# Query, key and value turns of a transformer block written out and skewed over the engines, with the norms ahead of them on VectorE

## The reference, cut to what matters

```python
ada = t_emb @ w_ada + b_ada
sh_msa, sc_msa, g_msa, sh_mlp, sc_mlp, g_mlp = jnp.split(ada, 6, axis=-1)
xn = layer_norm(logmap0(x))
xm = expmap0(xn * (1 + sc_msa) + sh_msa)
q = _to_heads(plin(xm, w_q, b_q))        # plin: expmap0(logmap0(x) @ w + b)
k = _to_heads(plin(xm, w_k, b_k))        # 16 heads of 16 columns, each rescaled
v = _to_heads(plin(xm, w_v, b_v))
scores = jnp.einsum('bhqd,bhkd->bhqk', logmap0(q), logmap0(k)) / math.sqrt(HD)
...
x = x + _L0_cond_ref(x, cond_1024[:, None, :], ...)
x = x + _L1_cond_ref(x, cond_1024, Wx, Wh, b)     # LSTM, 512 steps
```

## Time and profile before

| | us |
|---|---|
| median of three runs | 1699.41 |
| lowest, highest | 1697.03, 1707.28 |
| profiled execution | 1704.82 |
| its span, first to last instruction | 1703.1 |
| TensorE, VectorE, ScalarE, GpSimd busy | 1504.9, 1182.9, 915.1, 466.2 |
| mean granted TensorE clock, share of full | 0.901 |

### The profile page before, as it was taken

How to read it: one execution, slowest core, us unless ns; L and a number is a source line. 1 busy time by engine, 2 the same in 40 slices (tenths; PEclk the granted TensorE clock), 3 DMA queues, 4 the chain that set the end, 5 groups by cost and what they waited for, 6 DMA issues and landing times.

```text
span 1703.1 us, 65744 instructions
## 1 busy us (share of the span) xinstructions
PE 1504.9 (88%) x25387; PEld 1261.3 (74%) x25387; DVE 1182.9 (69%) x6690; ACT 915.1 (54%) x3335; POOL 466.2 (27%) x1246
## 2 busy tenths in 40 slices
PE   3565658548999999999999999999999999999998
PEld 3444546437887888888888888888788888888887
DVE  6465657636888787868786868677766767676665
ACT  0334349627676666565656565657454454544433
POOL 4222220200515142515151515151513314140100
PEclk9767675567999999989998989899999999999999
DMA  8000000000000000000000000000000000000000
GB/s 247 0 0 0 0 0 2 1 1 5 3 3 10 3 10 3 9 3 9 8 5 7 5 9 3 9 3 9 3 9 3 9 3 9 6 3 6 3 6 6
DMA packets 16711, 18.39 MB, mean 11 GB/s; under 512 B 6037, under 2 KB 15385, under 8 KB 16409
## 3 DMA queue, kind: packets, MB, share of 16 engines
q1 hardware_dynamic: 13016, 10.51, 2.1%
q10 hardware_dynamic: 3392, 3.81, 0.8%
HBM read 12.21 MB, written 2.10 MB: 8 GB/s over the span
## 4 chain that ended last, share of the span: by engine, by line
PE 64%; DVE 10%; POOL 4%; ACT 4%; issue 4%; POOLq 0%; ACTq 0%; DVEq 0%
PE psum L784 22%; PE psum L822 19%; PE psum L760 4%; PE psum L725 4%; PE psum L732 3%; PE psum L660 3%; DVE weights L1146 2%; POOL sc L262 2%; PE psum L672 2%; PE psum L740 2%; PE psum L774 2%; ACT weights L895 1%; DVE gA L1386 1%; DVE gF L1388 1%; POOL sc L464 1%
## 5 line engine op out<-in xcount | busy, mean ns | idle before, releaser
L784 PEld LDWEIGHTS psum<-hl,wh 128*128 128x128 f16 x16384 | 480.3, 96 | 86.0 <-DVE hl L1404 74.6
L784 PE MATMUL psum<-hl,wh 128*128 128x8 f16 x16384 | 515.9, 172 | 5.8 <-DVE hl L1404 3.7
L822 PE MATMUL psum<-zeros,ident 128*128 128x256 f16 x3316 | 451.5, 276 | 7.4 <-DVE gF L1388 2.1
L822 PEld LDWEIGHTS psum<-zeros,ident 128*128 128x128 f16 x3316 | 304.8, 98 | 79.4 <-DVE gF L1388 17.9
L992 ACT ACTIVATE tA<-gA 128x16 f32<-128x16 f32 x512 | 110.4, 216 | 434.1 <-DVE gA L1386 433.6
L1146 DVE TENSOR_TENSOR weights<-w,weights 128x256 f16<-128x256 f32 x512 | 202.9, 418 | 18.7 <-ACT weights L895 18.4
L1386 DVE TENSOR_REDUCE gA<-psum 128x16 f32<-128x32 f32 x512 | 96.5, 189 | 148.3 <-PE psum L784 141.6
L901 ACT ACTIVATE w<-psum 128x512 f32<-128x512 f32 x256 | 154.4, 603 | 4.9 <-DVE weights L1146 4.5
L1402 DVE TENSOR_TENSOR hl<-ot 128x8 f16<-128x8 f32 x512 | 90.1, 176 | 95.1 <-ACT ot L998 94.9
L895 ACT ACTIVATE weights<-psum 128x512 f16<-128x512 f32 x256 | 153.6, 600 | 3.9 <-PE psum L672 3.9
L998 ACT ACTIVATE ot<-cnew 128x8 f32<-128x8 f32 x512 | 109.6, 214 | 81.6 <-DVE cnew L1395 31.9
(11 more groups left out here) (301 smaller groups left out, 2318.2 us busy)
## 6 DMA issues: line engine op xcount, KB each, us to landing
arena<-in_x_dram SPq DMA_DIRECT2D x4, 512.0 KB, 9.6
wf<-in_L_cond_w_f_dram SPq DMA_DIRECT2D x2, 1024.0 KB, 17.2
xr<-in_x_dram SPq DMA_DIRECT2D x64, 32.0 KB, 1.8
out_dram<-place SPq DMA_DIRECT2D x64, 32.0 KB, 1.6
qTs<-in_L_cond_w_ada_dram ACTq DMA_DIRECT2D x1, 1536.0 KB
oT<-in_L_cond_Wh_dram ACTq DMA_DIRECT2D x1, 1024.0 KB, 14.1
wx<-in_L_cond_Wx_dram SPq DMA_DIRECT2D x1, 1024.0 KB, 18.8
rows<-in_L_cond_b_ada_dram ACTq DMA_DIRECT2D x4, 128.0 KB, 14.4
```

Of the source, the lines that this page charges most:

```text
L784: last = mm(cols, wh16[:, half, kc, (g0 + c) * P:(g0 + c + 1) * P], hl[:, :, kc, :, 2].rearrange("p e b -> p b e"), start=False, stop=c == ...
L822: mm(pF[:, D:2 * D], ident16[:], zeros[:], start=False, stop=False, skip_group_check=True)
```

## The change

The start and the loop are rewritten; attention, recurrence and output stay, but for buffer names. Four groups of edits:

1. **Norms.** `to_ratio` and `to_norm` are gone from GpSimd. VectorE computes them in `norms(tiles, part)`, four parts for tiles 0 to 3 and four for tiles 4 to 15, laid between the statistics, which now have three `mv6` buffers and no wait after each. GpSimd computes four powers.
2. **Smaller start.** `adac` has only the two parts that the loop needs (8 products, not 24). The other uses of w_ada, the products for h0, the maximum of W_h over partitions and the units move into `between_turns` of the engines. W_h's high halves are ScalarE's (`high_half`, turns 4 to 11), the low halves VectorE's, one instruction each after the loop.
3. **Written out and skewed.** The loops become Python loops over turns -3 to 17. In turn t TensorE does heads t-2, linears t+1, transpose t+3, norm column t+2; ScalarE squares t, modulation t+2, norm t+3, roots t, copies t-2; VectorE linears t, row norm t+1, factors t-1, head sums t, halves t-1; GpSimd row factor t+1, values t-1. `lin` and `uT` have two buffers.
4. **Wider instructions.** `lin` is one instruction of 768 columns from three banks; the factors f are one; q and k are one of 512. TensorE waits only for ld_q (w_q, w_k, w_v) ahead of the linears, and the biases are loaded ahead of W_h. The table load for the attention is at turn 15.

```diff
+for i, ((lo, hi), which) in enumerate((tiles, which) for tiles in (FIRST_TILES, LAST_TILES) for which in (HALF_UP, HALF_DOWN)):
+    hold(pool, "q_in", i + 1)
+    w = hi - lo
+    g.tensor_tensor(num(f"ka{lo}", w), num(f"kb{lo}", w), cst[:, which, 0:w], ALU.pow).then_inc(s["q_out"], 1)
+ch = Chain(pool, s["hsc"], s["held"], 0)
+def tile_scale(k):
+    hold(pool, "p_ns", k + 1)
     clip(ch, num("su"), num("nu"), 1, num("ca"), num("cb"), s["p_su"])
+def values(k):
     hold(pool, "p_f", k + 1)
+    ch.link(g.tensor_scalar(num("fv", H), num("f", 48)[:, 2 * H:3 * H], V_UP, None, ALU.mult))
...
+    hold(pool, "p_v", k + 1)
     g.tensor_copy(vh, v32).then_inc(s["p_vh"], 1)
     hold(pool, "p_vh", k + 1)
     g.tensor_tensor(vl, v32, vh, ALU.subtract).then_inc(s["p_vl"], 1)
+for turn in range(-1, NT + 1):
+    if turn + 1 < NT:
+        tile_scale(turn + 1)
+    if 0 <= turn - 1:
+        values(turn - 1)
...
+for turn in range(-3, NT + 2):
+    if 0 <= turn - 2:
+        heads_turned(turn - 2)
+    if 0 <= turn + 1 < NT:
+        linears(turn + 1)
+    if turn + 3 < NT:
+        x_turned(turn + 3)
+    if 0 <= turn + 2 < NT:
+        row_norm(turn + 2)
+    between_turns(turn)
+pe.wait_ge(s["ld_w"], 16 * WLOADS)
+pe.wait_ge(s["h0_s"], 1)
+pe.wait_ge(s["p_kc"], NT)
+pe.wait_ge(s["p_qc"], NT)
...
+def between_turns(turn):
+    if turn == 0:
+        pe.wait_ge(s["pk"], 1)
+        tr(bank[6][0:1, 0:P], big1[:, 2:3], ident[:]).then_inc(s["wmax"], 1)
+    if turn == 1:
+        pe.wait_ge(s["pk"], 2)
+        mm(bank[6][:, 256:257], ones[0:1, :], big1[0:1, 4:5], start=True, stop=True, skip_group_check=True).then_inc(s["wmax"], 1)
+    if turn in (3, 4, 6, 7):
...
+        for kc in range(KD):
+            last = mm(GROUP_ROWS[i % 2], c0R[:, kc, :, :].rearrange("p b t -> p (b t)"), wada[:, kc, part * D:(part + 1) * D],
+                      start=kc == 0, stop=kc == KD - 1, skip_group_check=True)
+        last.then_inc(s["gp"], 1)
+    if 9 <= turn < 13:
+        if turn == 9:
+            pe.wait_ge(s["ld_h"], 16)
+            pe.wait_ge(s["gp_s"], 2)
+        for gi in (2 * (turn - 9), 2 * (turn - 9) + 1):
+            c = CHUNK[gi]
+            for kc in range(KD):
+                last = mm(bank[6][:, gi * B:(gi + 1) * B], wh[:, kc, c * P:(c + 1) * P], c0T[:, kc, :],
+                          start=kc == 0, stop=kc == KD - 1, skip_group_check=True)
+        last.then_inc(s["h0p"], 1)
...
+def high_half(gi):
+    c = CHUNK[gi]
+    if gi == 0:
+        act.wait_ge(s["unit_s"], 1)
+    A(wh16[:, 0, :, gi * P:(gi + 1) * P], wh[:, :, c * P:(c + 1) * P], ACT.Copy,
+      scale=big1[:, 6:7] if UNIT[gi] == 1.0 else big1[:, 5:6]).then_inc(s["w_hi"], 1)
+logs(FIRST_TILES, 1)
+normed(0)
+for turn in range(-2, NT + 2):
+    if 0 <= turn < NT:
+        squares(turn)
+    if turn + 2 < NT:
+        modulated(turn + 2)
+    if turn + 3 < NT:
+        normed(turn + 3)
+    if turn == -2:
+        logs(LAST_TILES, 2)
+    if 0 <= turn < NT:
+        roots(turn)
+    if turn == NT - 1:
+        nc.scalar.preload_act_table_set("exp_and_others")
+    if 0 <= turn - 2:
+        heads_kept(turn - 2)
+    if 4 <= turn < 4 + GC:
+        high_half(turn - 4)
...
+def norms(tiles, part):
+    lo, hi = tiles
...
+    if part == 1:
+        link(d.tensor_tensor(N("a"), m, m, ALU.mult))
+        link(d.tensor_tensor(N("c"), N("a"), var, ALU.add))
+        d.tensor_scalar(N("b"), N("c"), float(D), None, ALU.mult).then_inc(s["q_in"], 1)
+    if part == 2:
+        v.wait_ge(s["q_out"], 2 * number + 1)
...
+    if part == 3:
+        v.wait_ge(s["lnr"], number + 1)
+        link(d.scalar_tensor_tensor(N("lam"), N("L"), 0.5, N("ndi"), ALU.mult, ALU.mult))
...
+        d.tensor_scalar(N("b"), N("d"), LN_EPS, None, ALU.add).then_inc(s["q_in"], 1)
+    if part == 4:
+        v.wait_ge(s["q_out"], 2 * number + 2)
+        link(d.tensor_tensor(kap[:, lo:hi], N("lamf"), N("a"), ALU.mult))
+        d.scalar_tensor_tensor(kmn[:, lo:hi], kap[:, lo:hi], -1.0, m, ALU.mult, ALU.mult).then_inc(s["ln1"], 1)
...
+statistics(0, 4)
+norms(FIRST_TILES, 1)
+statistics(4, 6)
 v.wait_ge(s["c0t"], 1)
 d.tensor_copy(c0T[:], bank[0][:, 0:KD * B].rearrange("p (k b) -> p k b", b=B)).then_inc(s["c0t_s"], 1)
+norms(FIRST_TILES, 2)
+statistics(6, 8)
 v.wait_ge(s["c0t_s"], 1)
 d.tensor_copy(c0R, c0T[:].unsqueeze(3).to_broadcast([P, KD, B, RING])).then_inc(s["c0t_s"], 1)
+norms(FIRST_TILES, 3)
+statistics(8, 11)
+norms(FIRST_TILES, 4)
+statistics(11, NT)
+norms(LAST_TILES, 1)
+v.wait_ge(s["adap"], 1)
+link(d.tensor_tensor(adac[:], bank[1][:, 0:2 * KD * B].rearrange("p (c b) -> p c b", b=B),
+                     badac[:, 0:2 * KD].unsqueeze(2).to_broadcast([P, 2 * KD, B]), ALU.add))
+d.tensor_scalar(adac[:, KD:2 * KD, :], adac[:, KD:2 * KD, :], 1.0, None, ALU.add).then_inc(s["ada_s"], 1)
+norms(LAST_TILES, 2)
 v.wait_ge(s["ld_h"], 16)
+d.tensor_reduce(big1[:, 0:1], wh, axis=AX.XY, op=ALU.max)
+norms(LAST_TILES, 3)
 link(d.tensor_reduce(big1[:, 1:2], wh, axis=AX.XY, op=ALU.min))
 link(d.tensor_scalar(big1[:, 3:4], big1[:, 1:2], -1.0, 2.0 ** -60, ALU.mult, ALU.max))
 d.tensor_tensor(big1[:, 2:3], big1[:, 0:1], big1[:, 3:4], ALU.max).then_inc(s["pk"], 1)
...
+def linears(k):
+    v.wait_ge(s["p_mm"], k + 1)
+    v.wait_ge(s["p_su"], k + 1)
+    if k == 0:
+        v.wait_ge(s["ld_bq"], 16 * 3)
+    if k >= 2:
+        v.wait_ge(s["p_v"], k - 1)
+    d.scalar_tensor_tensor(lin_of(k), psum[:, 2:5, 0:D], num("su"), bqkv, ALU.mult, ALU.add).then_inc(s["p_lin"], 1)
...
+def factors(k):
+    v.wait_ge(s["p_r"], k + 1)
+    link(d.tensor_scalar(num("ct", 3), num("rss", 51)[:, 48:51], REACH * HEAD, HEAD, ALU.mult, ALU.min))
+    if k >= 1:
+        v.wait_ge(s["p_v"], k)
+    by_three = lambda t: t.rearrange("p (a h) -> p a h", a=3)
...
+    v.wait_ge(s["p_f"], k + 1)
+    by_head = lambda t: t.rearrange("p a (h e) -> p (a h) e", e=HD)
+    d.scalar_tensor_tensor(by_head(qk), by_head(lin_of(k)[:, 0:2, :]), QK_UP,
+                           num("f", 48)[:, 0:2 * H].unsqueeze(2).to_broadcast([P, 2 * H, HD]), ALU.mult, ALU.mult).then_inc(s["p_qk"], 1)
+def head_sums(k):
+    v.wait_ge(s["p_sq"], k + 1)
+    if k >= 1:
+        v.wait_ge(s["p_r"], k)
+    d.tensor_reduce(num("ss", 51)[:, 0:48], tmp[:, 0:3 * D].rearrange("p (h e) -> p h e", e=HD), axis=AX.X, op=ALU.add).then_inc(s["p_s1"], 1)
+    v.wait_ge(s["p_s1"], k + 1)
+    link(d.tensor_reduce(num("ss", 51)[:, 48:51], num("ss", 51)[:, 0:48].rearrange("p (a h) -> p a h", a=3), axis=AX.X, op=ALU.add))
+    d.tensor_scalar(num("ss", 51), num("ss", 51), 1.0, None, ALU.max).then_inc(s["p_ss"], 1)
...
+for turn in range(-1, NT + 1):
+    if 0 <= turn < NT:
+        linears(turn)
+    if turn + 1 < NT:
+        row_norm(turn + 1)
+    if 0 <= turn - 1:
+        factors(turn - 1)
+    if 0 <= turn < NT:
+        head_sums(turn)
+    if 0 <= turn - 1:
+        halves(turn - 1)
+    between_turns(turn)
+v.wait_ge(s["h0p"], 4)
+v.wait_ge(s["unit_s"], 1)
...
+v.wait_ge(s["w_hi"], GC)
+for gi, c in enumerate(CHUNK):
+    d.scalar_tensor_tensor(wh16[:, 1, :, gi * P:(gi + 1) * P], wh[:, :, c * P:(c + 1) * P],
+                           big1[:, 6:7] if UNIT[gi] == 1.0 else big1[:, 5:6], wh16[:, 0, :, gi * P:(gi + 1) * P],
+                           ALU.mult, ALU.subtract).then_inc(s["w_lo"], 1)
```

More of the change, by code:

```diff
@@ L583, in _ @@
             pe.wait_ge(s["c0t_s"], 2)
-            for c in range(6 * KD):
+            for c in range(2 * KD):
                 for kc in range(KD):
@@ L588, in _, with x_turned @@
             last.then_inc(s["adap"], 1)
-            pe.wait_ge(s["pk"], 1)
-            tr(bank[6][0:1, 0:P], big1[:, 2:3], ident[:]).then_inc(s["wmax"], 1)
-            pe.wait_ge(s["pk"], 2)
-            mm(bank[6][:, 256:257], ones[0:1, :], big1[0:1, 4:5], start=True, stop=True).then_inc(s["wmax"], 1)
-            for i, part in enumerate((2, 5, 4, 3)):
-                for kc in range(KD):
-                    last = mm(bank[2 + i // 2][:, (i % 2) * D:(i % 2 + 1) * D], c0R[:, kc, :, :].rearrange("p b t -> p (b t)"),
-                              wada[:, kc, part * D:(part + 1) * D], start=kc == 0, stop=kc == KD - 1, skip_group_check=True)
-            last.then_inc(s["gp"], 1)
-            def norm_x(k, first):
+            def x_turned(k):
                 pe.wait_ge(s["p_xn"], k + 1)
-                if not first:
+                if k >= 1:
                     pe.wait_ge(s["p_uT"], k)
@@ L1038, in link, with statistics @@
                 v.wait_ge(s["vchain"], nv)
+            def statistics(first, last):
+                nonlocal nv
+                before = nv
+                for k in range(first, last + 1):
+                    if k < last:
+                        if k % B == 0:
+                            v.wait_ge(s[f"ld_x{k // B}"], 16)
+                        if k >= first + 3:
+                            v.wait_ge(s["vchain"], before + 2 * (k - first) - 3)
+                        d.bn_stats(mv6[:, k % 3, :], xin[:, k, :]).then_inc(s["vchain"], 1)
```

(15 more changed lines are left out.)

354 lines of the change are left out of this document (149 added, 205 removed).

## The result

The changed kernel takes 1602.3 us (median, 1597.9 to 1603.7), the kernel before beside it 1703.4: a ratio of 0.940, 95% interval 0.938 to 0.942. The forecast was 1619, in a range of 1602 to 1641, so the direction and the places of the gain were right, and the gain was larger, 101 us for 80. The profiled execution took 1597.9 us with a span of 1596.2.

What follows compares the result with a forecast made beforehand. It took a ring of waits ahead of the attention, not an engine, as the bound. Start 36.7, 15 turns of 7.5, extras 9.0 and 1.8, then the seam put the first exponential 80.4 us earlier: 1619 us, range 1602 to 1641.

Steps and rivals of the forecast that it cites:

- The bound of before and the path: Ahead of 254.6 us: a chain of waits repeating every 12.0 us, no engine full; time saved there comes off the end.
- The start: Ahead of the loop: norms on VectorE bring the first linears to 36.7 us from 54.1, a gain of 17.4.
- VectorE's turn: VectorE's work in one turn of the new loop: 5.8 to 6.8 us, taken as 6.8.
- TensorE's turn: TensorE as longest engine of the new loop: 9.1 us at half clock, some 5.2 at full, taken as 7.5.
- the ring: The old loop over sixteen tiles: a closed chain of waits through the engines, repeating every 12.0 us.
- All counted: Group and h0 products moved into the turns cost their whole 9.0 us, since TensorE is longest; turn 0's wait adds 1.8.
- The seam: From tile 15's linears to the attention's first exponential: 14.2 us, with the 1.28 table load moved to turn 15.
- The loop branch: The old loop's taken branch loses VectorE nothing that a wait doesn't explain, so writing it out gains nothing by itself.
- A: Rival: TensorE stays at the half clock through the loop, turn 9.1, 24 us more, 1643; chance 0.15.
- B: Rival: an in-order queue closes the ring again despite the skew, turn near 12, 1679; chance 0.06.
- C: Rival: the clock falls in more stretches of the recurrence, 7.1 us each, 114 us in all, 1733; chance 0.04.

Runs made afterwards that it cites:

- the experiment: Changed kernel with ScalarE's copies of tile 13 put ahead of the roots of tile 15 and the table load: 1601.3 us, ratio 0.939.

## Why the prediction was right and wrong

- **The bound of before and the path.** Right. All of the gain lies ahead of the first exponential, and the rest runs as before but for 1.5 us.
- **The start.** Right within 1.7: forecast 36.7, measured 34.99. The row copy stands at 33.04 for the 35.0 of the sum, and the linears 1.95 behind it for 1.7. The two powers, the two reductions (2.29 and 2.28) and the end of TensorE's linears (31 and 31.1) came out as priced. The experiment with the norms on GpSimd gives 16.3 of the 17.4 forecast.
- **VectorE's turn.** Within its bounds (5.8 to 6.8), 6.2, where I took 6.8. The low end of the range was made with that 6.8 as the shortest turn, which is 9 us over fifteen turns, and this is why the result could come out at its edge. The wide linear is 1.00 as taken, the cast to stack 0.72 as forecast. What was too dear is everything but the halves, 3.9 with the linear: it takes 3.4 (106.91 to 110.27). The halves are 2.8 (110.27 to 113.10, where the next linears start), for 2.9.
- **The step that failed: TensorE's turn, "I take 7.5", the longest engine.** I averaged the two levels as the ring had mixed them, though the edit removes the idle times that went with the low one. Measured: clock 1.00 in three of the four turns shown, linears 2.83, norm product 0.50, transpose 0.38, heads 0.62 and 0.61: 4.9, near the 5.2 that I had worked out for the full clock. With that VectorE is the longest engine, and the turn 6.2: tripling TensorE's norm products left most turns as they were, while every change of VectorE's time showed in them. TensorE was busy for 0.81 of the loop (78.52 of 96.70), not over nine tenths. From 36.7 and 34.99 the loop took 96.7 where I had 123.3: 15 x (7.5 - 6.2) = 19.5 is this term.
- **"All counted": the 9.0 of TensorE's extras and the 1.8 of turn 0.** This followed from the same choice and fell with it. The turns with group products or h0 products are no longer than others; in their place VectorE's own pieces cost (7.38 in turn 2, 6.86 in turns 5 and 8), and turn 0, with a wait of 3.7, lasted 7.47. Together the loop exceeds 15 x 6.19 by 3.9, for 10.8 forecast: 6.9 us of the error.
- **The seam.** 14.46 for 14.2. The table load was not free at turn 15, as I had it: it stood ahead of a copy for which TensorE and then VectorE waited. That cost 0.8 in the experiment, and the last halves, which met GpSimd's work only in their first cast, took 1.8 and not 2.8 (140.40 to 142.22), which gives back 1.0.
- **The loop branch.** The branch itself is free at its place, as I had read. The conclusion, that writing out gains nothing by itself, is wrong: 8.6 us in the ring, 7.1 of it on ScalarE, whose operands with a register are worked out behind the release. I had looked at VectorE's branch alone. The Trainium skill ("Runtime: NRT & Kernel Launch", Instruction fetch mechanics) says that a taken branch can force a fetch stall; the gain has its sign, but no row shows it at the branch.
- **The rivals.** A (half clock): the clock in the last of these turns averages 0.72 and the turn stays 6.19, but with less work for TensorE, so that turn alone doesn't say what the low clock would have cost; the tripled norm products, at 0.87, cost 2.9 us. B: no; C: no, the recurrence is 1291.4 for 1288.9.

The sum of the errors at the first exponential: 1.7 + 19.5 + 6.9 - 0.3 = 27.8 of 28.05 (174.2 - 146.15).

## What to carry to other kernels

When an edit opens a ring of waits, don't price TensorE with the clock that the ring was granted: work the turn out at both levels, and see which engine is longest at each, since the new order may be granted the full one (0.69 before, 0.92 after). Then every term that hung on the longest engine (extras, waits, pieces) has to be worked out again for the other candidate, because they are counted or hidden together. And where VectorE binds, GpSimd's work beside it has a price that is read from the same instruction's short and long duration; moving it earlier pays only if what it also delivers (here the row factor) doesn't become late.

## What the runs showed of the hardware that was not expected

- ScalarE's instructions in a hardware loop started 0.33 (kT) and 0.18 us (modulation) later behind a release than the same ones written out, because its sequencer worked out their addresses only then (register operations of 207 and 35 ns, and of 74 to 118); behind a running instruction the same kind of work cost nothing. TensorE's loop, without a register in its operands, cost nothing (254.6 and 254.6).
- GpSimd is blocked too: its one-column power took 0.88 beside VectorE's multiply L1182 in the changed kernel and 0.57 where it met the linears instead; its one-column clip step went from 0.23 to 0.74. VectorE's multiply (0.69) and head sums (0.94 to 0.95) kept their durations in each of these.
- Work added to TensorE can be worth time: with 21 idle products a turn in the ring the granted clock was 0.88 for 0.73, and the first exponential came 8.9 us earlier. It isn't so everywhere: with the norm's one-column products tripled in the skewed loop the clock was 0.87 for 0.92, and the exponential came 2.9 later.
